# Relational graph convolution on Trainium2: longer edge rows whose self loops are squeezed out on VectorE, and where the edges are loaded

## The chip, the cores and the metric
The kernel runs on one core of a Trainium2 chip. The core has five engines that run programs of their own and wait for each other by semaphores: TensorE (PE, with its weight loads shown apart as PEld), VectorE (DVE), ScalarE (ACT), GpSimd (POOL) and SyncE (SP, which here only issues DMAs), and 16 DMA engines that move the data. The metric is the time of one launch in microseconds (us), the median over runs; lower is better.

## The reference
6250 nodes with 128 features, 106250 edges sorted by destination: 50000 random pairs in both directions and one self loop (source = destination) for each node, which stands last among the edges of its node. Every edge has one of 8 relations.

```python
def _layernorm(x, axis=-1, eps=1e-05):
    m = jnp.mean(x, axis=axis, keepdims=True)
    v = jnp.var(x, axis=axis, keepdims=True)
    return (x - m) / jnp.sqrt(v + eps)
...
h = jnp.maximum(_layernorm(x, axis=-1), 0.0)
out = h @ W_root + bias
for r in range(num_rels):
    m = (edge_type == r).astype(x.dtype)
    msg = h[src] @ W[r] * m[:, None]
    agg = jax.ops.segment_sum(msg, dst, num_segments=n)
    cnt = jax.ops.segment_sum(m, dst, num_segments=n)
    out = out + agg / jnp.maximum(cnt, 1.0)[:, None]
return x + out
```

## The kernel before, in words
**Tiles and groups.** The edges are gathered in tiles of 128 rows of h: a tile is one indirect DMA that POOL issues (L540, `hg<-h_table,src_i`), one source node per partition. Self loops need no gather, since h of the own node is at hand. So the kernel takes *rows* of edges longer than a tile: the first 48 rows have 128 edges, all others 133 (RAW = 128 + SPARE), and the self loops among a row's 133 edges are replaced by its 5 last edges, so that 128 are left for the tile. That gives TILES = 801 tiles, in GALL = 267 groups of GT = 3. Five groups are an iteration, in which one block of BLK = 116 nodes is finished; there are 54.

**A group's way.** POOL gathers its three tiles; DVE makes three one-hot matrices (L1048); PE multiplies them with the gathered rows into `acc` (L1560, and L1564 for the counts); ACT makes the one-hot of the group's self loops (L653, L656), which PE adds as counts (L1567); DVE adds `acc` to a ring of sums over nodes and relations (L1062). For each block DVE then puts the self loops' h in (`make_block`, L1097 and L1103), PE multiplies with the eight W (L1591), DVE adds the terms, divided by the counts (L1146), and SP stores the 116 rows of the output (L436). Tiles are gathered ahead into slots: the gather of group g waits until group g-10 is summed (`user_before`). Two groups are not gathered by POOL but fetched row by row by SP (FETCHED).

**The start.** The 24 tiles of the first XG = 8 groups are gathered from x itself and normalised tile by tile, while h = relu(layernorm(x)) is computed for all nodes on DVE and ACT (L611), nine chunks and a rest, and stored to a table in DRAM (L416, L418). The gather of tile 24 is the first that reads this table: POOL waits there for all stores (L528).

```python
            load_x(0)
            load_x(1)
            sp.wait_ge(pads, 4)
            chunks(1, dst)
            load_x(2)
            load_x(3)
            chunks(2, etype)
            for k in range(4, NORM_STEPS):
                load_x(k)
            chunks(0, src)
            for k in range(NORM_STEPS):
                at = slice(NORM_CUTS[k], min(NORM_CUTS[k + 1], LC))
                sp.wait_ge(h_ready, NORM_CUTS[k + 1])
                sp.dma_start(table_rows[:, at, :], h_all[:, at, :]).then_inc(h_stored, 16)
```

All of this is in SP's queue in the order written (L403 to L418). `chunks` loads dst, type or src as rows of edges on partitions; `load_x` loads nodes, 128 partitions each.

**The preparation of the rows** (`run_ends`, `ranks_and_words`, `spare_into_hole`, L863 to L958) is DVE's: keys, ranks of the self loops, and one word per edge out of key and source, in which the self loops are overwritten. The 126 first rows are done before the loop, the other 675 in three parts during iterations 3 to 14, in steps of 2 x 133 elements per partition (PARTS).

Of the kernel before, what the change touches and what calls it, by code (L numbers as in the profile page):

```python
# [8 lines left out]
P = 128  # L9
F = 128  # L10
R = 8
N = 6250
E = 106250
WHOLE = 48
SPARE = 5
RAW = P + SPARE
TILES = WHOLE + ceil((E - WHOLE * P) / RAW)
# [4 lines left out]
ITERS = ceil(TILES / IT)  # L22
BLOCKS = ceil(N / BLK)
LAG = 2
GALL = ceil(TILES / GT)
ENDG = (ITERS - 1) * GROUPS
# [3 lines left out]
EARLY = ENDI * GROUPS  # L30
# [7 lines left out]
FETCHED = (209, 264)  # L38
FETCH = 16
FETCH_FROM = 7  # L40
# [6 lines left out]
RC = 126  # L47
RG = RC // GT
CHUNKS = ceil(TILES / RC)
ROWS_L = TILES - (CHUNKS - 1) * RC  # L50
# [24 lines left out]
EDGES_L = E - start_of(TILES - 1)  # L75
PRE = -window(0)[0]
WINDOWS = [tuple(PRE + at for at in window(j)) for j in range(GT)]
WINN = WINDOWS[-1][1]
RINGW = PRE + RING * BLK + WINN
WIN = WINN * R  # L80
OHW = max(b - a for a, b in WINDOWS) * R
# [15 lines left out]
SLOTS = 32  # L97
ABOVE = 4096.0
LOOP_FLAG = 1024.0
PARTS = ((0, 1), (1, 2), (3, 2), (5, 2))  # L100
PART_GROUPS = [c0 * RG for c0, n in PARTS]
PART_FROM = 3
PART_ITERS = 4
STATICS = PART_FROM + PART_ITERS * (len(PARTS) - 1) + 2
CHECKS = 4 * len(PARTS) + 6
RAW_TILES = ceil(E / P)
RAW_LAST = E - (RAW_TILES - 1) * P
assert WINN == 32 and BLOCKS == ITERS and GALL * GT == TILES and GALL == ENDG + 2 and CH * LOADS == BLOCKS
assert XG * GT > IT and XG <= 2 * GROUPS and N < 1 << NODE_BITS and WHOLE >= XG * GT and RC % GT == 0 and ROWS_L % GT == 0


def rgcn(nc, x, src, dst, etype, w, w_root, bias, out):
# [5 lines left out]
    with ExitStack() as ctx:  # L118
# [6 lines left out]
        def sem(name):  # L125
# [20 lines left out]
        e_rows_i = sb("e_rows_i", [RC, 3, CHUNKS, RAW + 1], i32)  # L146
        e_rows = sb("e_rows", [RC, 3, CHUNKS, RAW + 1])
        row_at = sb("row_at", [RC, CHUNKS])
        off1 = sb("off1", [RC, CHUNKS])
        off2 = sb("off2", [RC, CHUNKS])  # L150
        off = sb("off", [RC, CHUNKS])
        rank_from = sb("rank_from", [RC, CHUNKS])
        minus_base = sb("minus_base", [RC, CHUNKS])
        heads = sb("heads", [RC, CHUNKS, RG])
        lead = sb("lead", [RC, RG, GT])
        ends = sb("ends", [RC, 2, RAW])
        near_key = sb("near_key", [RC, 2, RAW])
        loop_val = sb("loop_val", [RC, 2, RAW])
        loop_rest = sb("loop_rest", [RC, 2, RAW])
        rank = sb("rank", [RC, 2, RAW])  # L160
        words = sb("words", [RC, 2, RAW])
        fill = sb("fill", [RC, 2, 2, P])
        unequal = sb("unequal", [RC, 2, RAW])
        top = sb("top", [RC, CHUNKS, SLOTS])
        words_i = sb("words_i", [P, 2 * RC], i32)
        key_i = sb("key_i", [P, 2 * RC], i32)
        src_i = sb("src_i", [P, CHUNKS * RC], i32)
        key_f = sb("key_f", [P, CHUNKS * RC])
        loop_key = sb("loop_key", [GT * SLOTS, CHUNKS * RG])
        base = sb("base", [P, max(CHUNKS * RG, ITERS * GROUPS)])  # L170
        near = sb("near", [P, ITERS * GROUPS])
        laps = sb("laps", [P, GALL])
# [36 lines left out]
        row_bad = sb("row_bad", [RC, 4, CHUNKS])  # L209
        row_ok = sb("row_ok", [RC, CHUNKS])  # L210
        row_gap = sb("row_gap", [RC, 4, CHUNKS])
# [18 lines left out]
        late_src = e_rows_i[:, :, :, :].rearrange("p a c w -> p (a c w)")[0:1, 0:2 * P]  # L230
# [20 lines left out]
        eps_made, ones_made, zeros_made, ring_cleared, top_made = (  # L251
            sem("eps_made"), sem("ones_made"), sem("zeros_made"), sem("ring_cleared"), sem("top_made"))
# [52 lines left out]
        def tiles_in(i, q):  # L305

            return GT if not isinstance(i, int) else max(0, min(GT, TILES - i * IT - q * GT))
# [1465 lines left out]
```

## Time and profile before

| | |
|---|---|
| time, median of 3 runs | 1021.49 us (1020.2 to 1022.13) |
| profiled execution | span 1020.0 us on the device, the sum of what lies in the profile; no time beside the span is given for it, and it lies 0.2 us under the lowest of the runs and 1.5 us under their median |
| busy, of that span | PE 769.5 us (75%), POOL 757.4 (74%), DVE 706.0 (69%), ACT 413.9 (41%) |
| DMA | 53978 packets, 71.57 MB |

Busy shares say how long an engine executed instructions; time in which it issues a DMA or handles a semaphore is not in them. So 74% for POOL does not say that it waited for the other 26%.

### The profile page before, as it was taken

How to read it: one execution, taken by the hardware profiler on the slowest of the kernel's cores; microseconds unless marked ns; L12 is line 12 of the kernel's file. 1: busy time of each engine (PE TensorE's matmuls, PEld its weight loads, DVE VectorE, ACT ScalarE, POOL GpSimd, SP SyncE). 2: the span in 40 equal slices, each digit the busy share in tenths (PEclk: the TensorE clock that was granted, in tenths of full speed). 3: DMA queues.
4: the chain of work that ended last, by engine and by line, in shares of the span. 5: the costliest groups of instructions: out<-in, count | busy, mean ns of one | idle time of the engine just before them, and what ended most of it. 6: DMA issues, size and time to landing. Idle time of an engine off the chain costs nothing.

```text
span 1020.0 us, 17379 instructions
## 1 busy us (share of the span) xinstructions
PE 769.5 (75%) x4342; PEld 634.1 (62%) x4342; DVE 706.0 (69%) x2309; ACT 413.9 (41%) x821; POOL 757.4 (74%) x808
## 2 busy tenths in 40 slices
PE   0488786887888777877877868878778687787787
PEld 0277675675666665655756756657657566675676
DVE  7798978768776767576666566665765756657676
ACT  7985253352343342432432423423424334243242
POOL 7677777777777777777777777777777777777772
PEclk9996767667676776676676676676766867667679
DMA  9694222222222222222222222222222222222221
GB/s 275 185 226 92 55 58 55 57 57 55 57 56 58 58 58 58 55 59 58 57 56 58 58 55 60 56 58 59 55 59 57 56 60 56 57 58 56 59 57 29
DMA packets 53978, 71.57 MB, mean 70 GB/s; under 512 B 15523, under 2 KB 39110, under 8 KB 53878
## 3 DMA queue, kind: packets, MB, share of 16 engines
q0 software_dynamic: 25440, 52.15, 20.2%
q1 hardware_dynamic: 28438, 18.30, 7.0%
q8 instruction: 37, 0.61, 0.3%
q14 instruction: 63, 0.52, 0.2%
HBM read 63.99 MB, written 6.40 MB: 69 GB/s over the span
## 4 chain that ended last, share of the span: by engine, by line
POOL 52%; issue 19%; PE 14%; DVE 6%; DMA 4%; ACT 4%; SPq 1%; DVEq 0%; POOLq 0%
POOL hg L540 52%; PE acc L1560 5%; PE fin L1591 4%; DMA hg<-h_table,src_i 4%; PE zp L1580 1%; ACT h_all L611 1%; DVE x_all L1146 1%; PE zp L1598 1%; DVE onehot L1048 1%; ACT hg L639 1%; PE acc L1567 1%; PE acc L1564 1%; DMA x_all<-in_x 1%; PE zp L1597 1%; DVE ring L1062 1%
## 5 line engine op out<-in xcount | busy, mean ns | idle before, releaser
L540 POOL DMA_INDIRECT hg<-h_table,src_i x771 | 732.6, 950 | 237.2 <-issue 229.2
L1560 PE MATMUL acc<-onehot,hg 128*128 128x96 f32 (+1 forms) x1602 | 408.3, 367 | 200.7 <-DMA hg<-h_table,src_i 168.4
L1560 PEld LDWEIGHTS acc<-onehot,hg 128*128 128x128 f32 x1602 | 320.9, 249 | 278.6 <-issue 207.1
L1062 DVE TENSOR_TENSOR ring<-ring,acc 128x512 f32 x267 | 181.8, 681 | 239.2 <-PE acc L1567 229.5
L663 ACT ACTIVATE hT<-zp 128x116 f32<-128x116 f32 x50 | 13.4, 267 | 516.3 <-PE zp L1598 516.0
L1048 DVE TENSOR_SCALAR onehot<-iota,key_f 128x96 f32<-128x96 f32 (+1 forms) x801 | 197.2, 293 | 11.4 <-issue 2.6
L1564 PE MATMUL acc<-onehot,ones_bf 128*128 128x96 bf16 (+1 forms) x801 | 204.0, 255 | 0.0
L1591 PE MATMUL fin<-w_sb,blk 128*116 128x128 f32 x800 | 179.3, 398 | 0.0
L1591 PEld LDWEIGHTS fin<-w_sb,blk 128*116 128x116 f32 x800 | 161.6, 288 | 11.9 <-issue 11.7
L653 ACT ACTIVATE loop_far<-iota,loop_key 96x256 f32<-96x256 f32 x267 | 134.0, 502 | 40.9 <-PE acc L1567 28.7
L1146 DVE SCALAR_TENSOR_TENSOR x_all<-fin,inv,x_all 116x128 f32<-116x128 f32 x400 | 139.1, 348 | 14.4 <-DVE x_all L1136 0.5
L656 ACT ACTIVATE loophot<-loop_far,ones 96x256 bf16<-96x256 f32 x267 | 135.6, 508 | 8.7
L1564 PEld LDWEIGHTS acc<-onehot,ones_bf 128*128 128x128 bf16 x801 | 117.5, 147 | 0.0
L1567 PE MATMUL acc<-loophot,flags_bf 96*128 96x256 bf16 x267 | 91.2, 341 | 0.9 <-ACT loophot L656 0.9
L675 ACT ACTIVATE ring<-zeros 128x928 f32<-128x928 f32 x98 | 89.6, 962 | 0.0
L1103 DVE TENSOR_TENSOR blk<-ring,fin 128x464 f32<-128x464 f32 x100 | 63.8, 638 | 10.6 <-DVE fin L1097 0.5
L1097 DVE SCALAR_TENSOR_TENSOR fin<-ring,zp 128x464 f32<-128x464 f32 x100 | 64.1, 641 | 1.7
L1580 PEld LDWEIGHTS zp<-ident,ring 1*116 1x116 f32 x400 | 42.1, 203 | 20.3 <-issue 14.4
L1580 PE MATMUL zp<-ident,ring 1*116 1x1 f32 x400 | 46.3, 232 | 4.9 <-DVE fin L1097 4.9
L1567 PEld LDWEIGHTS acc<-loophot,flags_bf 96*128 96x128 bf16 x267 | 32.7, 122 | 13.3 <-ACT loophot L656 1.1
L1598 PE MATMUL zp<-bias_sb,ones 1*116 1x128 f32 x100 | 37.9, 480 | 0.0
L1597 PE MATMUL zp<-wr_sb,hT 128*116 128x128 f32 x100 | 31.2, 414 | 0.0
(152 smaller groups left out, 369.1 us busy)
## 6 DMA issues: line engine op xcount, KB each, us to landing
hg<-h_table,src_i POOLq DMA_INDIRECT x771, 2.5
hg<-h_table SPq DMA_DIRECT2D x768, 0.5 KB
out<-x_all SPq DMA_DIRECT2D x53, 58.0 KB
x_all<-in_x SPq DMA_DIRECT2D x7, 384.0 KB, 7.9
h_table<-h_all SPq DMA_DIRECT2D x7, 384.0 KB
h_all<-h_table SPq DMA_DIRECT2D x5, 504.0 KB
x_all<-in_x SPq DMA_DIRECT2D x5, 504.0 KB
w_sb<-in_L_gnn_W SPq DMA_DIRECT2D x1, 512.0 KB
```

Source lines behind the costliest of these rows:

```text
L540: nc.gpsimd.indirect_dma_start(out=hg[:, slot_of(t), :], out_offset=None, in_=x if g < XG else table, in_offset=bass.IndirectOffsetOnAxis( ...
L653: nc.scalar.activation(loop_far[:, :], iota[0:GT * SLOTS, :], ACT.Abs, bias=loop_key[:, bass.ds(g, 1)], scale=-1.0).then_inc(loop_far_read ...
L656: nc.scalar.activation(loophot[:, q, :], loop_far[:, :], ACT.Relu, bias=ones[0:GT * SLOTS, 0:1], scale=-1.0).then_inc(loophot_ready, 1)
L675: nc.scalar.activation(ring[:, a, :, slot], zeros[:, :].rearrange("p (r n) -> p r n", r=R), ACT.Copy).then_inc(slot_clear, 1)
L1048: nc.vector.tensor_scalar(onehot[:, t, 0:(e - a) * R].rearrange("p (r n) -> p r n", r=R), by_node[:, :, a:e], key_f[:, bass.ds(i * IT + t, ...
L1062: nc.vector.tensor_tensor(ring[:, :, :, at], ring[:, :, :, at], acc[:, q, :, :].rearrange("p a (r n) -> p a r n", r=R), ALU.add).then_inc( ...
L1146: nc.vector.scalar_tensor_tensor(out=x_b, in0=fin[0:BLK, r // (R // 2), at:at + F], scalar=inv[:, r:r + 1], in1=x_b, op0=ALU.mult, op1=ALU ...
L1560: nc.tensor.matmul(both[:, 0, :, a:e], hg[:, slot, :], hot.rearrange("p (r n) -> p r n", r=R), start=(j == 0), stop=(j == n - 1), skip_gro ...
L1564: nc.tensor.matmul(both[:, 1, :, a:e], ones_bf[:, :], halves, start=False, stop=False, skip_group_check=True)
L1567: nc.tensor.matmul(acc[:, q, 1, :], flags_bf[:, :], loophot[:, q, :], start=False, stop=True, skip_group_check=True).then_inc(group_summed, 1)
L1580: last = nc.tensor.transpose(cntT[:, r:r + 1], ring[0:1, 1, r, at:at + BLK], ident[0:1, 0:1])
L1591: last = nc.tensor.matmul(fin[0:BLK, r // (R // 2), at:at + F], blk[:, r, :], w_sb[:, r, :], start=True, stop=True)
```

## The change
Only the first 126 rows stay as they were. Behind them stand 42 rows of 403 edges (LONG_A), each of which yields 3 tiles (384 edges, 19 spare), and 90 rows of 809 edges (LONG_B), each of which yields 6 tiles (768 edges, 41 spare). A longer row needs fewer spare edges for each tile, so there are 792 tiles in place of 801, 264 groups in place of 267. The three groups that are gone are taken from the front (G0 = 3): iteration 0 has only its last two groups, and from there each place in the program holds what it held before.

The self loops are no longer overwritten by spare edges but squeezed out: every word carries in its top bits how many self loops stand before it, and for each bit of this number a mask is made and all words with the bit set move by 1, 2, 4, 8, 16 (and 32) places to the front, in `COPY_PREDICATED`. That is 5 moves for A and 6 for B, after some ten other operations over the full width of 403 or 809 elements. The steps of A run in iterations 3 to 6, those of B in 8 to 11, five per iteration (`long_work`), then the words are transposed and split as before. More groups get a one-hot of another width (windows of 12 to 16 nodes in place of 12, 12 and 17).

```diff
+LONG_A = Long(42, 3, 19, 5, (138,), RC, FIRST_EDGES, 1)
+LONG_B = Long(90, 6, 41, 6, (138, 542), RC + LONG_A.rows * LONG_A.tiles, FIRST_EDGES + LONG_A.rows * LONG_A.width,
+              1 + LONG_A.tiles)
+G0 = VGROUPS - GALL
-FETCHED = (209, 264)
+FETCHED = (209 - G0, 264 - G0)
-FETCH_FROM = 7
+FETCH_FROM = 11
-PARTS = ((0, 1), (1, 2), (3, 2), (5, 2))
-PART_FROM = 3
-PART_ITERS = 4
+LONG_FROM = [3, 8]
...
-            def chunks(a, v):
-                w, done = RAW + (a == 1), edges_in[a]
-                sp.dma_start(e_rows_i[0:WHOLE, a, 0, 0:w], rows_of(v, 0, WHOLE, None, w, P)).then_inc(done, 16)
-                sp.dma_start(e_rows_i[WHOLE:RC, a, 0, 0:w], rows_of(v, WHOLE, RC - WHOLE, None, w)).then_inc(done, 16)
-                sp.dma_start(e_rows_i[:, a, 1:CHUNKS - 1, 0:w], rows_of(v, RC, RC, CHUNKS - 2, w)).then_inc(done, 16)
-                sp.dma_start(e_rows_i[0:ROWS_L - 1, a, CHUNKS - 1, 0:w],
-                             rows_of(v, RC * (CHUNKS - 1), ROWS_L - 1, None, w)).then_inc(done, 16)
+            def edge_rows(a, v):
+                more, done = a == 1, edges_in[a]
+                w = RAW + more
+                sp.dma_start(first_i[0:WHOLE, a, 0:w], rows_of(v, 0, WHOLE, w, P)).then_inc(done, 16)
+                sp.dma_start(first_i[WHOLE:RC, a, 0:w], rows_of(v, WHOLE * P, RC - WHOLE, w, RAW)).then_inc(done, 16)
+                w = LONG_A.width + more
+                sp.dma_start(long_i[0][:, a, 0:w], rows_of(v, LONG_A.first_edge, LONG_A.rows, w, LONG_A.width)).then_inc(done, 16)
+                w, rows = LONG_B.width + more, LONG_B.rows - 1
+                sp.dma_start(long_i[1][0:rows, a, 0:w], rows_of(v, LONG_B.first_edge, rows, w, LONG_B.width)).then_inc(done, 16)
+                sp.dma_start(long_i[1][rows:rows + 1, a, 0:LAST_ROW],
+                             rows_of(v, E - LAST_ROW, 1, LAST_ROW, LAST_ROW)).then_inc(done, 16)
...
+                def move(bit):
+                    def step():
+                        by = 1 << bit
+                        counted(nc.vector.tensor_scalar(one_i[:, by:], word_i[:, by:], SHIFT_AT + bit, 1,
+                                                        ALU.arith_shift_right, ALU.bitwise_and))
+                        prep_done()
+                        counted(nc.vector.copy_predicated(word_i[:, 0:w - by], one_i[:, by:], word_i[:, by:]))
+                        prep_done()
+                    return step
...
+                return [run_ends_of_long, keys_of_long, differ, ends_extremes, differ_extremes, loop_values, first_tops,
+                        without_first_tops, second_tops, loops_before, whole_words, shifts_into_words,
+                        *[move(bit) for bit in range(v.bits)], plain_words, words_to_turn]
+
+            def long_work(i, q):
+
+                for k, since in enumerate(LONG_FROM):
+                    at = 5 * (i - since) + (0, 0, 1, 3, 5)[q]
+                    if since <= i and 1 <= q <= 3:
+                        for step in long_steps(k)[at:at + (0, 1, 2, 2, 0)[q]]:
+                            step()
```

On SP, near the start of the program, this stands before, from the second load of x on (`x_all`) over the loads of dst to the first of the edge types; the numbers at a row's end are partitions x elements, and x2 says that the row stands twice:

```order
L396 DMA x_all<-in_x 128x768
L382 DMA e_rows_i<-in_dst 48x134
L383 DMA e_rows_i<-in_dst 78x134
L384 DMA e_rows_i<-in_dst 126x5x134
L385 DMA e_rows_i<-in_dst 44x134
L387 DMA e_rows_i<-in_dst 1x90
L396 DMA x_all<-in_x 128x768 x2
L382 DMA e_rows_i<-in_edge_type 48x133
```

Most of the edges are in the one load of 126 partitions with five rows on each. At the same place on SP there is now:

```order
L468 DMA x_all<-in_x 128x768
L453 DMA first_rows<-in_dst 48x134
L454 DMA first_rows<-in_dst 78x134
L456 DMA long_rows<-in_dst 42x404
L458 DMA long_rows<-in_dst 89x810
L459 DMA long_rows<-in_dst 1x805
L468 DMA x_all<-in_x 128x768 x2
L453 DMA first_rows<-in_edge_type 48x133
```

The number of loads, their place in the queue and nearly all their bytes are the same; two loads of 126 and 44 partitions have become loads of 42 and 89 partitions with long rows. The same holds for the types and the sources that follow.

On DVE, in iteration 10, a stretch of the program before reads as follows; `fill` and `words` belong to the preparation, `onehot` and `ring` to the groups:

```order
L894 SCALAR_TENSOR_TENSOR fill<-rank,words 126x256
L898 TENSOR_TENSOR words<-words,fill 126x2x128 [waits prep_step]
L1048 TENSOR_SCALAR onehot<-iota,key_f 128x96 [waits prep_step]
L1048 TENSOR_SCALAR onehot<-iota,key_f 128x96
L1048 TENSOR_SCALAR onehot<-iota,key_f 128x136
L1062 ISA [waits group_summed,group_added]
L1062 TENSOR_TENSOR ring<-ring,acc 128x16x32
```

Two operations of the preparation stand between two groups there. In the same place of iteration 10 the change has, with `long_rows` and `scratch` for the preparation of LONG_B:

```order
L1127 TENSOR_SCALAR scratch<-scratch 90x809
L1129 TENSOR_TENSOR long_rows<-long_rows,scratch 90x809 [waits prep_step]
L1135 TENSOR_SCALAR scratch<-long_rows 90x808 [waits prep_step]
L1138 COPY_PREDICATED long_rows<-scratch,long_rows 90x808 [waits prep_step]
L1250 TENSOR_SCALAR onehot<-iota,key_f 128x96 [waits prep_step]
L1250 TENSOR_SCALAR onehot<-iota,key_f 128x112
L1250 TENSOR_SCALAR onehot<-iota,key_f 128x128
L1264 ISA [waits group_summed,group_added]
L1264 TENSOR_TENSOR ring<-ring,acc 128x16x32
```

Four operations about three times as wide have taken the place of the two.

On POOL there is one row for the gathers from the table in each program, of before:

```order
L540 DMA hg<-h_table,src_i 128x128 x771
```

It stands for all tiles from the 25th on but those that SP fetches. On POOL of the change there is:

```order
L612 DMA hg<-h_table,src_i 128x128 x762
```

The nine tiles that are gone are nine gathers of POOL; those from x are 24 in both.

## Rows read from the trace of the kernel before

**Rows 1.** The page: span, busy time of each engine, and the chain that ended last.
```profile
span 1020.0 us, 17379 instructions
...
PE 769.5 (75%) x4342; PEld 634.1 (62%) x4342; DVE 706.0 (69%) x2309; ACT 413.9 (41%) x821; POOL 757.4 (74%) x808
...
POOL 52%; issue 19%; PE 14%; DVE 6%; DMA 4%; ACT 4%; SPq 1%; DVEq 0%; POOLq 0%
```

**Rows 2.** The page's groups: count, busy us, mean ns; idle time before and its releaser.
```profile
L540 POOL DMA_INDIRECT hg<-h_table,src_i x771 | 732.6, 950 | 237.2 <-issue 229.2
```

**Rows 3.** Waits of POOL: line, releaser, us in total, times, longest.
```profile
POOL hg L540 <- PE acc L1567: 5.5, 18, 0.3
```

**Rows 4.** Timeline of POOL: start, duration, what; two stretches.
```profile
32.30 0.94 POOL L540 DMA_INDIRECT hg<-in_x,src_i  x1 [0.30 <-issue]
35.77 0.94 POOL L540 DMA_INDIRECT hg<-h_table,src_i  x1 [2.52 <-DMA h_table<-h_all]
...
1002.12 0.94 POOL L540 DMA_INDIRECT hg<-h_table,src_i  x1 [0.31 <-issue]
```

**Rows 5.** Gathers and loop sums (L1567) of the span's first 500 us.
```profile
L540 POOL DMA_INDIRECT hg<-h_table,src_i x370: 940/944/1207, 35.8 to 499.5; - x185
...
L1567 PE MATMUL acc<-loophot,flags_bf x130: 275/280/420, 41.9 to 497.5; 96*128 96x256 bf16 x130
```

**Rows 6.** DMA of 1014.7:1015.7 and 1018.2:1018.9: last two stores (116 and 102 rows).
```profile
DMA packets 120, 0.06 MB, mean 59 GB/s; under 512 B 4, under 2 KB 120, under 8 KB 120
...
DMA packets 108, 0.05 MB, mean 75 GB/s; under 512 B 6, under 2 KB 108, under 8 KB 108
```

**Rows 7.** DMA of 26:31 and 17:22: packets, MB, share of 16 engines, by queue.
```profile
q1 hardware_dynamic: 375, 1.00, 50.8%
q0 software_dynamic: 157, 0.33, 24.8%
...
q1 hardware_dynamic: 1390, 1.30, 91.8%
q0 software_dynamic: 124, 0.23, 16.7%
```

**Rows 8.** Timelines of SP and ACT near the start: the loads, the last h.
```profile
2.70 0.44 SPq L382 DMA_DIRECT2D e_rows_i<-in_dst  x1
...
31.19 1.25 ACT L611 ACTIVATE h_all<-x_all,nmr,rstd 128x128 f32<-128x128 f32 x3
```

**Rows 9.** Gathers of 80.8:323.5 and of 322.9:563.6: count, min/median/max ns, first and last start.
```profile
L540 POOL DMA_INDIRECT hg<-h_table,src_i x193: 940/944/1207, 80.8 to 323.0; - x193
...
L540 POOL DMA_INDIRECT hg<-h_table,src_i x193: 940/944/1052, 323.0 to 563.2; - x193
```

**Rows 10.** Timeline of POOL and DVE, two places in which a gather took longer.
```profile
989.69 1.34 POOL L540 DMA_INDIRECT hg<-h_table,src_i  x1 [0.30 <-issue]
989.59 0.63 DVE L1307 SCALAR_TENSOR_TENSOR blk<-ring,tail_hT 128x464 f32<-128x464 f32 x1
...
14.61 1.14 POOL L540 DMA_INDIRECT hg<-in_x,src_i  x1 [0.30 <-issue]
14.32 0.62 DVE L972 CAST e_rows<-e_rows_i 126x938 f32<-126x938 int32 x1
```

**Rows 11.** DVE groups by shape: count, busy us, mean ns.
```profile
L1062 DVE TENSOR_TENSOR ring<-ring,acc 128x512 f32 x267 | 181.8, 681 | 239.2 <-PE acc L1567 229.5 <-issue 9.1
L898 DVE TENSOR_TENSOR words<-words,fill 126x256 f32<-126x256 f32 x15 | 6.4, 427 | 0.5
L882 DVE SCALAR_TENSOR_TENSOR words<-near_key,e_rows 126x133 f32<-126x133 f32 x1 | 0.3, 285 | 0.0
L981 DVE TENSOR_SCALAR e_rows<-e_rows_i 126x931 f32<-126x931 int32 x1 | 0.7, 707 | 0.0
```

**Rows 12.** Windows of 50 us: busy us (x instructions) of PE, PEld, DVE, ACT, POOL.
```profile
150.00:200.00 50.00, 37.11 (x205) 29.67 (x205) 40.85 (x124) 16.91 (x33) 37.84 (x40) 0.70 0.21 55
400.00:450.00 50.00, 37.88 (x205) 30.47 (x204) 31.24 (x96) 15.59 (x30) 37.81 (x41) 0.68 0.22 57
```

More of the change, by code:

```diff
@@ L167, in rgcn @@
[L167 to L170, printed above, removed]
+        first_i = sb("first_rows", [RC, 3, RAW + 1], i32)
+        long_i = [sb(f"long_rows{k}", [v.rows, 3, v.width + 1], i32) for k, v in enumerate(LONGS)]
+        first = first_i[:, :, :].bitcast(f32)
+        long = [v[:, :, :].bitcast(f32) for v in long_i]
+        scratch = sb("scratch", [P, 2, LONG_B.width + 1])
@@ new lines, in rgcn @@
+        long_node = sb("long_node", [LONG_B.rows, LONG_B.tiles, 2])
+        long_gap = sb("long_gap", [LONG_B.rows, LONG_B.tiles + 5])
+        long_bad = sb("long_bad", [LONG_B.rows, 4 * LONG_B.tiles + 8])
+        apart = sb("apart", [P, LONG_B.rows])
+        heads = sb("heads", [RC, GALL])
+        lead = sb("lead", [RC, RG, GT])
+        in_rows = lambda k, n: scratch[0:RC, 0, k * RAW:k * RAW + n]
+        ends, near_key, loop_val, loop_rest, rank, words = (in_rows(k, RAW) for k in range(6))
@@ L685, in iteration @@
                         tile_h(g)
-                    if static(i) and q == 1:
-                        for c in range(1, CHUNKS):
-                            typed_offsets(c)
+                    if g == 1:
+                        for part in range(1, len(PART_GROUPS)):
+                            typed_offsets(part)
                     if static(i, 1) and q == 3:
@@ L1511, in word_transposes @@
-            def word_transposes(part):
-                c0, n = PARTS[part]
-                pe.wait_ge(words_full, part + 1)
-                for k in range(n):
-                    last = nc.tensor.transpose(wordsT[:, k * RC:(k + 1) * RC], words[:, k, 0:P], ident[0:RC, 0:RC])
+            nc.tensor.matmul(baseT[:, 0:RG], ones[0:RC, :], heads[:, 0:RG], start=True, stop=True).then_inc(base_T, 1)
+            for v in LONGS:
+                at = slice(v.first_group, v.first_group + v.rows * v.groups)
+                nc.tensor.matmul(baseT[:, at], ones[0:v.rows, :], heads[0:v.rows, at], start=True, stop=True).then_inc(base_T, 1)
@@ new lines, in word_transposes @@
+            def word_transposes(e):
+                part, half = WORDS[e]
+                pe.wait_ge(words_full, part + 1)
+                if part == 0:
+                    nc.tensor.transpose(wordsT[:, 0:RC], words[:, 0:P], ident[0:RC, 0:RC]).then_inc(words_T, 1)
+                    return
+                n = LONGS[part - 1].rows
+                for j in range(GT):
+                    at = (half * GT + j) * P
+                    last = nc.tensor.transpose(wordsT[:, j * n:(j + 1) * n], long[part - 1][:, 2, at:at + P], ident[0:n, 0:n])
@@ L1517, in word_transposes @@
                 last.then_inc(words_T, 1)
             def loop_transposes(part):
-                c0, n = PARTS[part]
                 pe.wait_ge(top_full, part + 1)
-                pe.wait_ge(words_sb, part + 1)
-                for k in range(n):
+                pe.wait_ge(words_sb, PART_WORDS[part])
+                n, groups, at = (RC, 1, 0) if part == 0 else (LONGS[part - 1].rows, LONGS[part - 1].groups, LONGS[part - 1].top_at)
+                for g in range(groups):
                     for j in range(GT):
-                        last = nc.tensor.matmul(loopsT[j * SLOTS:(j + 1) * SLOTS, k * RG:(k + 1) * RG],
-                                                top[:, c0 + k, :], heads_of[:, :, j], start=True, stop=True,
+                        to, which = (slice(0, RG), heads_of[:, :, j]) if part == 0 else (slice(g * n, (g + 1) * n), ident[0:n, 0:n])
+                        last = nc.tensor.matmul(loopsT[j * SLOTS:(j + 1) * SLOTS, to],
+                                                top[0:n, at + (0 if part == 0 else g * GT + j), :], which, start=True, stop=True,
```

798 lines of the change are left out of this document (481 added, 317 removed).

## The prediction

> **What bounds the kernel now.** I began with the chain that ended last: more than half of it is POOL's gathers, and of the "issue" share most is what lies between them [rows 1]. POOL's busy share of 74% hides this, since it leaves out the time between two gathers. The page's group for L540 gives both: 0.95 us busy and 237.2/771 = 0.31 us idle, and the idle time is "issue", so POOL waits for nothing [rows 2]. From the first gather out of the table at 35.77 us to the last at 1002.12 there are 770 steps, 966.35/770 = 1.255 us each [rows 4]. POOL's waits for PE, which free its slots, come to 5.5 us in 18 times of at most 0.3 us, so that no buffer holds it up [rows 3]. So the time is three pieces: the start up to 35.77 us, 771 gathers, and 18 us behind the last one, in which PE, DVE and ACT finish the last blocks.
>
> In the first piece POOL is idle for 2.52 us, from the end of its 24th gather out of x to the landing of the last store of the table [rows 4]. What sets that moment at present is ACT: its last h is done at 31.19 + 1.25 = 32.44 us, and the last stores follow [rows 8].
>
> Next I asked how far POOL is ahead. In the first 500 us it gathered (24 + 370)/3 = 131 groups, while 130 groups had been summed [rows 5]. It may be 10 ahead. So about eight groups, 8 x 3.76 = 30 us, are left as a cushion: whatever delays PE or DVE by less than that in mid-span costs nothing.
>
> **What is removed.** Nine gathers: 9 x 1.255 = **-11.3 us** [rows 4]. The 18 us behind the last gather stay, since the groups dropped are the first ones and every place at the end holds the same work. The DVE, PE and ACT work of three groups is off the path.
>
> **What the loads do.** The order on SP shows the same loads at the same places, but three of 89 partitions with 3240 bytes each. I looked at how a transfer is divided among the 16 DMA engines. The profile counts one small packet for each engine that ends a transfer: the store of 116 rows of 512 B shows 120 packets, 4 of them under 512 B, and that of 102 rows shows 108 with 6 under 512 B [rows 6]. 4 is the largest divisor of 116 that is at most 16, and 6 is that of 102. So a transfer goes to as many engines as divide its number of rows. 126 rows went to 14 engines; 89 is a prime, and all 89 rows would go to **one** engine.
>
> The Trainium skill, "DMA: Bandwidth & Descriptors", section "Why a DMA increments its semaphore by 16 and not by 1", says so too: the largest k up to 16 that divides the slowest dimension of both sides is used. By that rule, the two stores above use 4 and 6 engines, and the trace agrees.
>
> No row shows one engine alone with such a load, so its price is an estimate. Between 26 and 31 us, with large packets, q1 moved 1.00 MB in 50.8% of 16 engines' 5 us: 1.00/(0.508 x 80) = 24.6 KB per us and engine [rows 7]. Between 17 and 22 us, with packets of 532 B, 1.30/(0.918 x 80) = 17.7 KB/us. A load of 89 x 3240 B = 288 KB takes 11.7 us at the first rate, 16.3 us at the second; packets of 3240 B are like the first, so I take 11.7, and three come to 35.2 us. Everything behind them in SP's queue has a share on this engine too, and its queue is worked off in order: x(2), x(3) behind dst, x(4) to x(8) behind the types, and the stores of the table behind the sources. So this engine's work until the table is stored is: start 2.8 us [rows 8]; x, 3.2 MB/16 = 200 KB, 8.1 us; the other edge rows, some 29 KB of small packets, 1.6 us; the single rows 0.4; the three loads 35.2; the table's 200 KB, 8.1. That makes 56.2 us. POOL's 24 gathers out of x share the engine: between 0.167 and 0.248 of its time while they run at 1.25 us [rows 7], 5.0 to 7.4 us, middle 6.2. So the first gather out of the table starts at 62.4 us in place of 35.77: **+26.6 us**. POOL has nothing else to do meanwhile, and the cushion lies behind it, not before it, so all of this is on the path. The bounds: without POOL's share 56.2 (+20.4); at 17.7 KB/us for the three loads and 7.4 for POOL, 77.3 (+41.5).
>
> What else waits for these loads: ACT's h needs x(4) to x(8), which lands from 36 to 41 us, and 28 of its operations at 1.25/3 = 0.42 us follow [rows 8], so it is done near 49 us, before the stores' turn at 52. The words of the first 126 rows need the sources at 52.7 us (their wait counts all five loads); at the present pace of this chain the first group is summed about 11 us later, near 64 us, and POOL needs that for its tenth group at 62.4 + 6 x 1.25 = 70. Hidden, with 6 us to spare.
>
> **What the preparation does to POOL.** POOL's pace is not the same everywhere: from 80.8 to 323.0 us, while the rows are prepared, 192 steps take 242.2 us, afterwards 240.2 [rows 9]. The 2.0 us are a few gathers that last longer, and each has a DVE operation over it that began just before and reads two operands from SBUF, or converts: a gather of 1.34 us at 989.69, with one of 0.63 us from 989.59 to 990.22, and one of 1.14 at 14.61 under a CAST that ends at 14.94 [rows 10]. The gather waits until the DVE operation ends. An operation that starts at any moment of the gather's period of 1.25 us thus costs on average about (d-0.08)²/(2 x 1.25). The 53 or so old operations of 0.43 us [rows 11] give 2.4 us by it, where 2.0 are seen: factor 0.86. For the new widths, 133 elements took 0.285, 256 0.427, 512 0.681 us, some 0.15 + 1.04 ns per element: 403 gives 0.57 us and 809 gives 0.99 us. B has 14 such operations (6 of them COPY_PREDICATED, which no row shows; I take it like the others), each 0.33 us: 4.6. A has 13, each 0.095: 1.2. Shifts, masks and casts with one operand go by 0.707 us for 931 elements [rows 11]: 0.63 and 0.385 us, together 1.65. The sum, 7.5 x 0.86 = 6.4, less the 2.0 that go away, is **+4.4 us**; bounds +2 (only A's and B's two-operand operations, in gaps) and +10 (COPY_PREDICATED at twice the time: 6 x (1.9²/2.5 - 0.33) = 6.7 more, times 0.86).
>
> The Trainium skill, "SBUF — State Buffer", section "Who interferes with whom", calls the port that VectorE and GpSimd share an exclusive lock for the whole instruction. By it the gather would wait in just this way, and the trace agrees.
>
> **The sum.** 1020.0 for the profiled span, + 26.6 - 11.3 + 4.4 = 1039.7; the median of the runs lies 1.49 above this span, so **1041 us**, 2% slower.
>
> **The rivals.**
> *The loads are hidden* (the other side): they go to all engines as before, because a row of 3240 B is cut up before it is divided, or the engine takes them aside from the others. Then 1021.5 - 11.3 + 4.4 = 1014.6 us, 0.7% faster. For it: the bytes are the same and the page's DMA share is low after the start. Against it: the count of ending packets. It decides if the table is stored less than 6.9 us later than now (11.3 - 4.4). Chance 0.11.
> *DVE becomes the bound in iterations 8 to 11.* An iteration is 18.8 us. DVE is busy 31.24 of 50 us without preparation [rows 12], 11.7 us of 18.8; a fourth of B's some 30 us comes to 7.6 more: 19.3. So DVE falls behind by 0.5 us per iteration, 2 to 3 us in all, more with COPY_PREDICATED at twice the time (+6). The cushion is 30 us. To decide, each of the four iterations must take 8 us more than that, B's steps twice as long as I think; then some 5 to 30 us come on top, 1046 to 1071. Chance 0.05, mostly above my range.
> *The single engine is slower than the large packets show*, at the second rate: + 13.7 us, 1055. It is in the first case's tail; chance 0.06 above 1052.
> *The loads are on few engines, not one, or partly overtaken*: +10 us in place of 26.6, 1025. Chance 0.04.
>
> **How the numbers follow.** The likeliest case, one engine, has 0.74 between 1031 and 1052 (bounds 20.4 and some 37 on the start, +2 to +7 on the ports), and its centre is 1041. Faster and slower are told apart at 0.2%, about what a measurement of this kernel can resolve: faster 0.12 (the hidden loads), same 0.01, slower 0.87.
>
> **What would show it.** In the changed trace: the table's first gather near 62 us, POOL idle 30 us before it, released by the table's store; the DMA share low (mostly one engine in 16) between 10 and 50 us; 762 gathers after it at 1.251 us outside iterations 3 to 11, and longer gathers, up to 1.9 us, beside COPY_PREDICATED; POOL's waits for PE about as now. Wrong would be a first table gather before 43 us, or POOL waiting for PE near 200 to 280 us.

## The result

The changed kernel takes 1044.55 us (median of 4 runs, 1043.81 to 1044.98), where the kernel before, on the same chip, took 1021.81: ratio 1.0222, 95% interval 1.0208 to 1.0237. It is 2.2% slower; 1041 had been forecast. The profiled execution took 1044.91 us with a span of 1042.9.

The page of the changed kernel: span, busy times, the chain that ended last, and the group of POOL's gathers.

```profile
span 1042.9 us, 17316 instructions
...
PE 764.3 (73%) x4301; PEld 628.1 (60%) x4301; DVE 720.7 (69%) x2370; ACT 410.9 (39%) x811; POOL 754.9 (72%) x799
...
POOL 53%; issue 19%; PE 9%; DVE 8%; DMA 5%; SPq 4%; ACT 2%; DVEq 0%; POOLq 0%
...
L612 POOL DMA_INDIRECT hg<-h_table,src_i x762 | 729.8, 958 | 261.9 <-issue 228.3
```

Against [rows 1, 2], nine gathers are gone, and their idle time has grown by 25 us. Its waits (releaser, us in total, times, longest), and the timeline at the seam between the gathers from x and those from the table, say where:

```profile
POOL hg L612 <- issue: 235.3, 772, 0.3
POOL hg L612 <- DMA h_table<-h_all: 29.9, 1, 29.9
POOL hg L612 <- PE acc L1816: 3.7, 12, 0.3
```

```profile
32.57 0.94 POOL L612 DMA_INDIRECT hg<-in_x,src_i  x1 [0.30 <-issue]
63.45 0.94 POOL L612 DMA_INDIRECT hg<-h_table,src_i  x1 [29.93 <-DMA h_table<-h_all]
```

It is one wait of 29.93 us, where there were 2.52 [rows 4]; behind it the gaps are the usual 0.30 us, those put down to PE too (3.7 us in 12 times). The first gather out of the table starts at 63.45 us in place of 35.77. That is +27.7 us. What comes after the seam is shorter: the last gather starts at 1024.26, so 761 steps take 960.8 us, where 770 took 966.35: -5.5 us. Behind the last gather lie 18.6 us in place of 17.9: +0.7. The three make 22.9 us, the difference of the spans. The last gather in the timeline:

```profile
1024.26 0.94 POOL L612 DMA_INDIRECT hg<-h_table,src_i  x1 [0.30 <-issue]
```

Why the table is late stands in SP's queue (start, duration of the issue, number of DMAs) and in the landing of the last load of 89 rows, as the chain gives it. (The chain goes on from there through VectorE's words of the first rows; that POOL itself waits for the table is what its waits show.)

```profile
4.01 0.25 SPq L458 DMA_DIRECT2D long_rows<-in_dst  x1
4.31 0.45 SPq L459 DMA_DIRECT2D long_rows<-in_dst  x1
4.81 3.50 SPq L468 DMA_DIRECT2D x_all<-in_x  x2
...
11.62 1.70 SPq L458 DMA_DIRECT2D long_rows<-in_edge_type  x1
13.36 11.10 SPq L459 DMA_DIRECT2D long_rows<-in_edge_type  x1
...
35.26 0.35 SPq L458 DMA_DIRECT2D long_rows<-in_src  x1
35.65 7.10 SPq L459 DMA_DIRECT2D long_rows<-in_src  x1
```

```profile
35.65 19.66 DMA long_rows<-in_src
```

Of types and sources, the issue of the one row that follows the load of 89 rows takes 11.10 and 7.10 us, for a row of 3 KB: SP itself is held up. Behind the first load of 89 rows, that of dst, the same issue takes 0.45 us, and the two loads of x after it 3.50. Presumably the queue of the engine that is still at work has no room by then; no run tests this. The sources land at 35.65 + 19.66 = 55.3 us. How many engines work meanwhile can be read off the GB/s of the DMA view. Here are 36 to 41 us of the changed kernel, in 40 slices:

```profile
GB/s 65 155 116 26 26 26 26 33 26 26 26 26 26 26 26 26 26 26 25 25 25 25 25 25 25 25 25 25 25 25 25 25 25 25 49 25 25 25 25 25
```

From the fourth slice on mostly 25 to 26 GB/s: one engine at the 24.6 KB/us that the prediction had taken from packets spread over 16 [rows 7].

The loads also delay the normalisation, by more than the prediction said. VectorE where it begins with x(4), which it had waited for, and ACT's last h:

```profile
39.77 1.26 DVE L860 BATCH_NORM_STATS2 stats<-x_all 128x6 f32<-128x128 f32 x6 [12.06 <-DMA x_all<-in_x]
...
54.75 1.25 ACT L685 ACTIVATE h_all<-x_all,nmr,rstd 128x128 f32<-128x128 f32 x3
```

The last h is done at 56.00 us, 0.7 after the sources have landed; the prediction had it near 49.

The second term, the port, shows in the gathers that last longer than 0.94 us. POOL and DVE at two places in which LONG_B is prepared:

```profile
188.92 1.76 POOL L612 DMA_INDIRECT hg<-h_table,src_i  x1 [0.30 <-issue]
...
188.87 1.00 DVE L1084 TENSOR_TENSOR scratch<-scratch 90x809 f32<-90x809 f32 x1
...
229.30 1.41 POOL L612 DMA_INDIRECT hg<-h_table,src_i  x1 [0.30 <-PE acc L1816]
...
228.82 1.09 DVE L1138 COPY_PREDICATED long_rows<-scratch,long_rows 90x808 int32<-90x808 int32 x1
```

At 188.92 the operation ends at 189.87, 0.95 us after the gather's start, and the gather is 0.82 us longer than usual. At 229.30 it is COPY_PREDICATED, which ends 0.61 us after the start, and 0.47 are lost. What the gathers of the two stretches took:

```profile
L612 POOL DMA_INDIRECT hg<-h_table,src_i x147: 940/944/1760, 101.2 to 290.3; - x147
...
L612 POOL DMA_INDIRECT hg<-h_table,src_i x541: 940/944/1240, 290.3 to 966.5; - x181
```

With preparation 146 steps take 189.1 us, 1.295 each; without, 540 steps take 676.2, 1.252.

### The profile page after: what moved, and what is told of

It reads as the page before. It is cut to its first block, busy times and chain, and to the rows that moved or that the text cites. A ratio compares the mean times of both kernels' runs of the same rounds, so it can differ in the third digit from the quotient of the medians.

```text
span 1042.9 us, 17316 instructions
## 1 busy us (share of the span) xinstructions
PE 764.3 (73%) x4301; PEld 628.1 (60%) x4301; DVE 720.7 (69%) x2370; ACT 410.9 (39%) x811; POOL 754.9 (72%) x799
## 4 chain that ended last, share of the span: by engine, by line
POOL 53%; issue 19%; PE 9%; DVE 8%; DMA 5%; SPq 4%; ACT 2%; DVEq 0%; POOLq 0%
POOL hg L612 53%; PE acc L1809 3%; PE fin L1840 2%; DMA hg<-h_table,src_i 2%; DMA long_rows<-in_src 2%; DVE ring L1264 1%; SPq L459 1%; DVE onehot L1250 1%; SPq L468 1%; SPq L502 1%; DVE x_all L1348 1%; PE zp L1829 1%; ACT hg L717 1%; DMA x_all<-in_x 1%; DVE fin L1299 1%
## 5 line engine op out<-in xcount | busy, mean ns | idle before, releaser
L1809 PE MATMUL acc<-onehot,hg 128*128 128x96 f32 (+4 forms) x1584 | 410.0, 373 | 204.9 <-DMA hg<-h_table,src_i 154.3
L1250 DVE TENSOR_SCALAR onehot<-iota,key_f 128x96 f32<-128x96 f32 (+4 forms) x792 | 195.8, 292 | 10.1 <-issue 1.2
L1813 PE MATMUL acc<-onehot,ones_bf 128*128 128x96 bf16 (+4 forms) x792 | 202.4, 256 | 0.0
L1840 PE MATMUL fin<-w_sb,blk 128*116 128x128 f32 x800 | 170.6, 383 | 0.0
L1840 PEld LDWEIGHTS fin<-w_sb,blk 128*116 128x116 f32 x800 | 152.9, 275 | 12.0 <-issue 11.9
L1813 PEld LDWEIGHTS acc<-onehot,ones_bf 128*128 128x128 bf16 x792 | 113.0, 143 | 0.0
```

The source lines that it names most:

```text
L1250: nc.vector.tensor_scalar(onehot[:, slot_of_group(g) * GT + j, 0:(e - a) * R].rearrange("p (r n) -> p r n", r=R), by_node[:, :, a:e], key_ ...
L1809: nc.tensor.matmul(both[:, 0, :, a:e], hg[:, slot, :], hot.rearrange("p (r n) -> p r n", r=R), start=(j == 0), stop=(j == GT - 1), skip_gr ...
L1813: nc.tensor.matmul(both[:, 1, :, a:e], ones_bf[:, :], halves, start=False, stop=False, skip_group_check=True)
L1840: last = nc.tensor.matmul(fin[0:BLK, r // (R // 2), at:at + F], blk[:, r, :], w_sb[:, r, :], start=True, stop=True)
```

## The experiments

Each number beside a kernel's name is its median; "before" is the kernel before, timed on the same chip in the same rounds.

### Two cuts of the load of 89 rows

`a_80_9` and `a_86_3` differ from the change in these lines (and in the counts of the semaphore), the second with 86 in place of 80.

```diff
-                sp.dma_start(long_i[1][0:rows, a, 0:w], rows_of(v, LONG_B.first_edge, rows, w, LONG_B.width)).then_inc(done, 16)
+                for r0, r1 in ((0, 80), (80, rows)):
+                    sp.dma_start(long_i[1][r0:r1, a, 0:w],
+                                 rows_of(v, LONG_B.first_edge + r0 * LONG_B.width, r1 - r0, w, LONG_B.width)).then_inc(done, 16)
```

Expected of 80 and 9 rows:

> The change with one edit: each load of 89 rows of LONG_B is issued as two, of 80 and of 9 rows. Theory (the number of rows sets how many of the 16 DMA engines carry a load; 89 is prime, so one does): 80 rows go to 16 engines, 9 to 9, the table is stored near 36 us, as before the change, and the time falls by about 27 us to 1016 to 1019. Rival (the long rows of 3240 bytes are slow in themselves, or SP's queue is held up by something else that came with them): the bytes, rows and places in the queue are the same, so the table stays late, over 50 us, and the time stays within 10 us of 1044.6.

Measured: 1015.23 us (before 1022.1), ratio 0.9939, interval 0.9925 to 0.9952. POOL's gathers from the table, first and last start:

```profile
L614 POOL DMA_INDIRECT hg<-h_table,src_i x762: 938/944/1755, 34.1 to 993.2; - x191
```

The table is there 29.3 us sooner, and the kernel, with the same bytes and the same rows, is 0.6% faster than before the change instead of 2.2% slower.

Expected of 86 and 3 rows:

> The same with 86 and 3 rows: by the theory the largest divisor of 86 up to 16 is 2, so two engines carry half of a load each, and the work of the engine that is late last is 3 x 144 KB less 24.6 KB/us = 17.6 us shorter than with 89 rows: first gather out of the table near 46 us, time near 1027. Rival (any cut in two halves the trouble, or a cut removes it whatever its sizes): the same time as with 80 and 9 rows.

Measured: 1027.53 us, ratio 1.0048, interval 1.0033 to 1.0064. First gather out of the table at 46.8 us. The DMA view of the same stretch, 36 to 41 us, of this kernel:

```profile
GB/s 273 77 59 59 52 26 52 26 52 52 66 42 165 370 360 411 370 418 377 410 254 58 49 74 49 49 49 49 49 49 74 49 123 393 393 393 393 418 418 393
```

49 to 52 GB/s where two engines carry the load alone, twice the 25 of one. The rival by which any cut would do has fallen: the divisor of the number of rows sets the rate. In the changed kernel the division is 1, here 2, with 80 rows 16.

The time of 46.8 us was expected, but not by the way it came about. I had summed the work of the engine that is late last. The trace shows the last h at 43.39 us, and the table read 3.4 us later; where no load runs on one engine alone, before the change and in `a_80_9`, it is 3.3 and 2.9 us. So with two engines the loads seem to delay the table only by delaying x, for which VectorE waits 14.6 us in all:

```profile
DVE stats L862 <- DMA x_all<-in_x: 14.6, 3, 8.2
...
42.14 1.25 ACT L687 ACTIVATE h_all<-x_all,nmr,rstd 128x128 f32<-128x128 f32 x3
```

### The same fault in the kernel before

`b_113_13`: nothing of the change is in it, but one of its loads is cut so that one part has a prime number of partitions.

```diff
-                sp.dma_start(e_rows_i[:, a, 1:CHUNKS - 1, 0:w], rows_of(v, RC, RC, CHUNKS - 2, w)).then_inc(done, 16)
+                for r0, r1 in ((0, 113), (113, RC)):
+                    sp.dma_start(e_rows_i[r0:r1, a, 1:CHUNKS - 1, 0:w],
+                                 rows_of(v, RC + r0, r1 - r0, CHUNKS - 2, w)).then_inc(done, 16)
```

> The kernel before the change with one edit: each load of 126 partitions with five rows of 133 or 134 edges is issued as two, of 113 partitions (a prime) and of 13. Nothing of the long rows or their preparation is in it. Theory: one engine carries 113 x 5 x 536 bytes = 303 KB three times, 12.3 us each at 24.6 KB/us and 17 at the 17.7 KB/us of small packets: the table is stored at 62 to 80 us, time 1050 to 1066. Rival (the loss comes from the long rows, not from the division): 1021 to 1023.

Measured: 1059.54 us, ratio 1.0363, interval 1.0347 to 1.0379. POOL's wait for the table and the DMA view from 36 to 41 us:

```profile
POOL hg L542 <- DMA h_table<-h_all: 39.6, 1, 39.6
```

```profile
GB/s 21 21 17 33 13 17 21 21 17 21 21 21 17 21 21 21 17 21 21 21 17 21 21 17 21 21 21 17 21 21 21 34 145 102 64 128 55 21 26 21
```

Again one engine, and with packets of 536 bytes it moves 17 to 21 GB/s, near the 17.7 worked out from [rows 7]. That window was not one of small packets alone, though: its 1.30 MB in 1390 packets are 935 bytes each. The loss needs neither long rows nor a new preparation.

### The same loads in another order

`a_89_late` keeps all three loads of 89 rows, and moves those of types and sources (with those of LONG_A) behind the table's stores and the weights. The waits for them move along: ACT waits for the late loads at group 6, where it had its work on the types at group 1.

```diff
-            edge_rows(2, etype)
+            edge_rows(2, etype, long=False)
...
-            edge_rows(0, src)
+            edge_rows(0, src, long=False)
...
             sp.dma_start(bias_sb[:, :], bias.rearrange("(a n) -> a n", a=1)).then_inc(consts_in, 16)
+            edge_rows(2, etype, first=False)
+            edge_rows(0, src, first=False)
```

> The change with its loads of 89 rows as they are, one engine each; only their order in SP's queue is changed: types and sources of LONG_A and LONG_B are loaded behind the stores of the table and the weights, those of dst stay in front. Theory (what counts is the work in front of the table's stores on the one engine): of 56.2 us of work two loads, 23.5 us, are gone from there, the first gather out of the table is near 39 us and the time near 1020. Rival (a load on one engine holds up the whole queue or memory wherever it stands): the later loads are paid for elsewhere, time near 1044.

Measured: 1036.28 us (before 1023.35), ratio 1.0128, interval 1.011 to 1.0146: between the two. The order matters, but 16 us less than I expected were won. DVE's timeline where it begins with x(2), of this kernel and of `a_80_9`, and this kernel's waits of PE and POOL from 60 to 100 us:

```profile
23.23 0.87 DVE L867 BATCH_NORM_STATS2 stats<-x_all 128x6 f32<-128x128 f32 x4 [15.10 <-DMA x_all<-in_x]
```

```profile
9.95 1.26 DVE L862 BATCH_NORM_STATS2 stats<-x_all 128x6 f32<-128x128 f32 x6 [1.83 <-DMA x_all<-in_x]
```

```profile
PE acc L1817 <- ACT hg L723: 11.0, 3, 7.6
PE zp L1831 <- DMA h_all<-h_table: 6.6, 1, 6.6
...
POOL hg L618 <- PE acc L1824: 6.0, 4, 3.1
```

First, the one load of dst that stays in front holds up x(2): VectorE begins with it at 23.2 us, while with 80 and 9 rows it did at 9.95. That is 13.3 us, and the first gather out of the table, at 46.93 us, comes 12.8 later than there. Behind x the normalisation takes its own 24 us, whatever the DMA engines do meanwhile; I had counted only the work on the one engine (39 us). That is 8 of the 16 us. Second, the late loads are now in front of the blocks of h that PE needs for the first output, and of types and sources for which ACT waits: PE stands, POOL's slots do not come free, and POOL waits 6.0 us in four times. 1.5 us more lie behind the last gather (20.1 in place of 18.6); the rest, under 1 us, I have not looked for.

### The price of the port

Three kernels add to `a_80_9`, in iterations 20 to 33, work on VectorE that is of no use: the output does not depend on it. The first adds 56 operations of 809 elements, the second cuts each into three of 270 with a wait for each piece, the third cuts them without waits. The second is shown; `prep_done()` is the wait for the operation before, and the third has it only in front of the first piece.

```diff
+                if 20 <= i < 34 and q < 4:
+                    for c0, c1 in [(0, 270), (270, 540), (540, 809)]:
+                        a, b = (scratch[0:90, k, c0:c1] for k in (0, 1))
+                        prep_done()
+                        counted(nc.vector.tensor_tensor(a, a, b, ALU.add))
```

> The change with loads of 80 and 9 rows, with 56 operations added on VectorE that compute nothing of use: scratch = scratch + scratch over 90 x 809 elements, 1.0 us each, one behind the sums of each of four groups per iteration in iterations 20 to 33, where VectorE has 7 us to spare per iteration. Theory (a gather that begins under an operation with two SBUF operands waits for its end): 56 x 0.34 x 0.86 = 16 us on top of loads of 80 and 9 rows alone, 1031, if the moments are spread evenly; as they repeat from one iteration to the next, 5 to 30 us are possible. Gathers of up to 1.9 us in 500 to 760 us. Rival (VectorE's time is hidden as long as it is not the bound): 1015 to 1017.

> As x_whole, with each added operation cut into three of 270 elements, and VectorE waits for each piece's semaphore before the next. Theory (the gather waits for the end of the one operation that it begins under): 168 x 0.05 x 0.86 = 7 us over loads of 80 and 9 rows alone, no gather above 1.4 us; less than half of the price of x_whole, with more VectorE time. Rival (total busy time counts): more than x_whole.

> As x_thirds_w, but without the wait between the pieces, so that the three stand directly behind each other. Theory A (VectorE gives the port back at the end of every instruction): the same as x_thirds_w. Theory B (which one gather of 1.87 us in the version cut into pieces suggests: with no wait between them, the pieces keep the port from the first to the last): as x_whole or a little more, since the three together take longer than one; gathers of up to 2 us.

Measured: 1031.9 us whole (ratio 1.0083, interval 1.0065 to 1.0101), 1022.74 in thirds with waits (0.9993, 0.9982 to 1.0005), 1029.75 in thirds without (1.0069, 1.0051 to 1.0088). Against the 0.9939 of `a_80_9`, with 1023 us for 1: +14.7, +5.5 and +13.3 us, where 16, 7 and "as x_whole or a little more" were expected. POOL's gathers of 370 to 700 us in `a_80_9`, whole, thirds with waits, thirds without:

```profile
L614 POOL DMA_INDIRECT hg<-h_table,src_i x264: 940/944/1175, 369.3 to 698.9; - x132
```

```profile
L614 POOL DMA_INDIRECT hg<-h_table,src_i x252: 941/946/1771, 369.7 to 699.7; - x126
```

```profile
L614 POOL DMA_INDIRECT hg<-h_table,src_i x260: 941/947/1194, 369.9 to 699.7; - x130
```

```profile
L614 POOL DMA_INDIRECT hg<-h_table,src_i x254: 941/947/1910, 369.1 to 699.0; - x127
```

In the same 330 us POOL issues 12, 4 and 10 gathers fewer. VectorE had time to spare in all three, and the middle one gives it the most work of the three: it is not its busy time that costs, but how long it holds the port at a stretch. Both ways of cutting at one place, first without waits:

```profile
402.60 1.90 POOL L614 DMA_INDIRECT hg<-h_table,src_i  x1 [0.30 <-issue]
...
402.56 1.13 DVE L1169 TENSOR_TENSOR scratch<-scratch 90x270 f32<-90x270 f32 x3
```

and with them:

```profile
402.98 1.18 POOL L614 DMA_INDIRECT hg<-h_table,src_i  x1 [0.30 <-issue]
...
402.91 1.37 DVE L1168 TENSOR_TENSOR scratch<-scratch 90x270 f32<-90x270 f32 x3
```

Both gathers begin under the first of three pieces. Without waits the pieces overlap each other (3 x 0.43 in 1.13 us) and the gather waits until the third has ended, 1.09 us after its start; with waits it waits for the first alone.

`a_pieces` does the same to the change: 80 and 9 rows, and all two-operand operations of the preparation in pieces of up to 270, with a wait behind each only in COPY_PREDICATED, where one piece overwrites what the piece before has read.

```diff
-                        counted(nc.vector.copy_predicated(word_i[:, 0:w - by], one_i[:, by:], word_i[:, by:]))
-                        prep_done()
+                        for c in parts:
+                            to = min(c.stop, w - by)
+                            counted(nc.vector.copy_predicated(word_i[:, c.start:to], one_i[:, c.start + by:to + by],
+                                                              word_i[:, c.start + by:to + by]))
+                            prep_done()
```

> The change with loads of 80 and 9 rows and, as a second edit, all preparation operations of LONG_A and LONG_B with two operands from SBUF cut into pieces of at most 270 elements, one behind the other, the same work otherwise. Theory (a gather that begins under such an operation waits for its end, so its price grows with the square of the duration): B falls from 14 x 0.36 to 42 x 0.05, A from 13 x 0.1 to 13 x 0.07, together 3.0 us less than with loads of 80 and 9 rows alone, and no gather over 1.4 us in iterations 3 to 11. Rival (the gathers are slowed by VectorE's total busy time in these iterations): no faster, or slower by the 0.15 us that each added operation costs.

Measured: 1013.03 us (before 1022.1), ratio 0.991, interval 0.9896 to 0.9923; `a_80_9` had 0.9939, 0.9925 to 0.9952. So 2.2 us less by the medians, but the intervals lie edge to edge (0.9923 and 0.9925), single runs of the two overlap, and the spans of the two profiled executions, 1012.7 and 1012.4, do not show it. The expectation of no gather above 1.4 us failed: one of 1.87 us at 162.1 lies under the three pieces of L1084, which have no wait between them; that gather led to the third of the runs above. By the medians it is the fastest kernel of this study, 0.9% faster than before; that it is faster than `a_80_9` is not shown beyond doubt.

### Four runs on another chip

The last four kernels ran on a chip on which the kernel before takes 1233.63 us, 21% more than the 1021 to 1024 us of all runs above, so nothing of them is compared with the runs above. `a_pieces_w` is `a_pieces` with a wait behind every piece, and `a_all_pieces` cuts the operations of one operand too. `a_dst89` and `a_src89` have 80 and 9 rows but for one array each:

```diff
+                for r0, r1 in ((0, rows),) if a == 1 else ((0, 80), (80, rows)):
```

> The change with loads of 80 and 9 rows and its preparation operations with two SBUF operands in pieces of at most 270 elements, as in the version cut into pieces, and now VectorE waits for each piece before the next. Theory (without such a wait the port is kept from piece to piece): the 3 us that were expected from the cut come in full, 1012.2; no gather above 1.45 us in iterations 3 to 11. Rival (the wait changes nothing): 1013, as without it; within this measurement's uncertainty the two are hard to tell apart, so the long gathers in the trace decide.

> As the version before, with the shifts, masks and casts of one operand cut as well. Theory: eleven of 0.57 us in B and ten of 0.36 us in A cost some 1.3 us together, a third of it stays: 0.8 us faster, 1011.5. Rival (VectorE, by now at some 22 us of work per iteration of 18.8 in iterations 8 to 11, falls so far behind that POOL waits for sums): slower, with waits of POOL for PE of over 1 us near 200 to 250 us.

> The change with 80 and 9 rows for types and sources; only the load of dst has 89 rows. Theory A (only the sum of work on the one engine counts): 38.5 us in front of the table, its first gather near 39, time near 1020. Theory B (x(2) to x(8) land behind this load, and VectorE and ACT need 25 us from there to the last h): first gather near 46.5 us, time near 1028. The run with late loads gave 46.9 where A said 39, but it had other orders too.

> The change with 80 and 9 rows for dst and types; only the load of the sources has 89 rows. It stands behind all of x, so the normalisation is not held up; the table's stores are behind it. Both theories: its 11.7 us begin near 22 us, where the queue on the one engine would have been free, and end near 36; the stores' 8 us come partly behind it: first gather between 39 and 44 us, time 1020 to 1025. Together with the run on dst: the price of a load is what stands behind it, not its length.

Measured: 1237.96 us (ratio 1.003, interval 1.0001 to 1.0058), 1241.35 (1.0075, 1.0048 to 1.0102), 1245.31 (1.0086, 1.006 to 1.0111) and 1241.58 (1.0062, 1.0039 to 1.0085). POOL's waits in `a_pieces_w` there, and a place at its start on DVE:

```profile
POOL hg L614 <- remote: 173.3, 92, 3.0
POOL hg L614 <- PE acc L1840: 26.6, 22, 2.8
```

```profile
16.61 0.48 DVE L862 BATCH_NORM_STATS2 stats<-x_all 128x6 f32<-128x128 f32 x2 [0.82 <-issue]
17.34 0.48 DVE L862 BATCH_NORM_STATS2 stats<-x_all 128x6 f32<-128x128 f32 x2 [0.24 <-issue]
```

(The second fence is of `a_src89`.) On this chip operations that otherwise stand back to back have gaps in which their engine waited for nothing that the profile shows, and POOL waits 200 us (173.3 of them for a releaser that the profile can't name, "remote"). At 400 us of `a_pieces_w` 86 groups are gathered and 77 added to the ring, and POOL may be 10 ahead: its lead is used up, so presumably a gather more or less no longer moves the end. As timings of the edits the four are inconclusive. Two things can be read within them all the same: in `a_pieces_w` no gather of the table lasts over 1.23 us, as expected of the waits, while `a_dst89`, which has its operations uncut, has some of up to 1.76; and the first gather out of the table starts at 56.2 us with the one load of dst, at 51.9 with the one of the sources, at 52.1 and 51.2 with neither. That is one trace each. It suggests that on that chip too the load in front of x costs (VectorE begins with x(2) at 24.6 us, and near 10 in the other three), and the one behind x nothing that can be seen; but there the normalisation was late already, and what the load of the sources alone costs where a launch takes 1022 us was not measured.

## Why the prediction was right

**The bound, and the nine gathers.** As forecast, POOL is back to back from the first gather out of the table to the last. The 11.3 us come in full, and are eaten in part by the port.

**The loads.** The main term was +26.6 us and measured +27.7. That the number of rows sets the number of engines, and that this makes the table late, is shown three times: by the ladder of 1, 2 and 16 engines (63.5, 46.8 and 34.1 us for the first gather out of the table), by the kernel before with a prime number of partitions, and by the even 25, 50 and 20 GB/s. By the rule of the Trainium skill ("DMA: Bandwidth & Descriptors", section "Why a DMA increments its semaphore by 16 and not by 1") 86 rows use two engines; the trace agrees, with 49 to 52 GB/s. The working was a sum of all that the one engine has to do, and for the changed kernel that is what decides: the sources landed at 55.3 us, and the 8.1 us of the table's share on this engine lead to the 63.45. (The prediction wrote 52.7 for the sources in one place; its own sum gives 62.4 - 8.1 = 54.3.) But one step beside the sum was wrong: the last h was forecast for 49 us and came at 56.00. The prediction had let ACT's 28 operations follow each other at 0.42 us, 11.8 us in all; from x(4) on, VectorE's moments and its preparation stand between them, and it took 16.2 (39.77 to 56.00). The total did not suffer only because the engine's 8.1 us for the table were still to come. From the last h to the first gather out of the table it was 7.4 us here, and 2.5 to 3.4 where the normalisation decides (before the change, `a_80_9`, `a_86_3`, `a_89_late`); so that path alone would have led to about 59 us, an estimate. Two delays of some 23 and of 27.7 us thus ran side by side, and the prediction had seen the longer one only; with some 5 us more on the other, its number would have failed. To that extent the close agreement is luck. In `a_86_3` and in the run with another order the normalisation does decide, and the sum is not valid: what stands in front of x costs its length again through the normalisation.

The late first groups did not become a wait, as forecast: PE had summed the first group at 67.0 us (64 forecast), and POOL needed its slot at 71.11 (70 forecast), so 4 us were to spare and not 6.

**The port.** Forecast +4.4. In the stretch of the preparation a step is 0.043 us longer than outside; over 146 steps that is 6.3 us, less the 2.0 of before [rows 9]: 4.3. In all, the gathers behind the seam took 5.8 us more than nine fewer should (11.3 less 5.5); the remaining 1.5 are spread over the rest, where a step is 1.252 in place of 1.251 us, and over the last iterations. COPY_PREDICATED over 808 elements took 1.10 us, 11% more than the line that I had laid through other operations, and it holds up the gather like they do. The factor on which the forecast rests was written as 0.86, where 2.0/2.4 is 0.83; that makes 0.2 us.

**The sum and the rivals.** 27.7 - 5.5 + 0.7 = 22.9 us measured in the spans, 19.7 forecast; the 3.2 us between are the start (1.1), the port (1.4) and the end (0.7). *The loads are hidden* was the right description of the kernel with 80 and 9 rows, for which it gave 1014.6 us; 1015.23 were measured (its table was read 1.7 us sooner than before the change and its end took 1.3 us longer, which nearly cancel). *DVE becomes the bound* did not occur: VectorE was busy 18.8 to 19.1 of each 20 us from 175 to 255 us, and yet at 190 us 41 groups had been gathered and 38 added to the ring, where POOL may be 10 ahead.

## What to carry to other kernels

Before a load or store is cut along partitions, look at the largest divisor up to 16 of its number of rows: 89 rows instead of 90, left over when one short row was split off, cost 29 us of 1015, and cutting them as 80 and 9 gave it back. What such a transfer costs is what stands behind it, both in its queue and in the engines that work on what comes late: here one load in front of x(2) alone cost 12.8 us, so look for the load that starts the longest chain, and what stands in front of it. Where GpSimd sets the pace, wide VectorE operations with two operands in SBUF are not free even if VectorE has time: keep them short, with a wait between them (56 operations cost 14.7 us whole and 5.5 us in thirds with waits).

## What the runs showed of the hardware that I had not expected

VectorE operations that follow each other without a wait keep GpSimd out from the first to the last: a gather under three pieces of 0.43 us lasted 1.90 us, and 1.18 us when each piece was waited for; 56 such triples cost 13.3 us and 5.5 us. The Trainium skill ("SBUF — State Buffer", section "Who interferes with whom") calls the shared port pair an exclusive lock, and says of VectorE's two-port modes that whoever issues first gets it for the whole instruction; for an instruction with two SBUF inputs it says only that it contends with GpSimd's reads. Here a single one of these held up the gather almost to its end (0.82 us lost under an operation with 0.95 us to go), and for several in a row the measurement goes further than the page.

Loads that use one engine held up the issuing engine too: behind the second of them SP needed 11.10 us for the issue of a load of 3 KB, and 0.25 us in `a_80_9`:

```profile
8.10 0.25 SPq L461 DMA_DIRECT2D long_rows<-in_edge_type  x1
```
